# Gate loops of a graph network by units of 1536 columns: one sigmoid per unit into SBUF, products in place on two engines

## The reference, cut to what matters

```
def _gate(h, q, Wg, bg, Wq, bq):        # B=8, N=32 nodes, L=64 queries, F=768
    hg = jnp.einsum('bnf,gf->bng', h3, Wg[:, :F])
    qg = jnp.einsum('blf,gf->blg', q, Wg[:, F:]) + bg
    attn = jax.nn.sigmoid(hg[:, :, None, :] + qg[:, None, :, :])
    qi = jnp.einsum('bnlf,blf->bnf', attn, q)
    alpha = jax.nn.sigmoid(h3 @ Wq[:, :F].T + qi @ Wq[:, F:].T + bq)
    hn = alpha * jnp.tanh(qi) + (1.0 - alpha) * h3
```

## Time and profile before

| what | value |
|---|---|
| time, median of 3 runs (lowest, highest) | 1493.0 us (1488.9, 1496.4) |
| the profiled execution: span from the first to the last instruction | 1493.6 us |
| PE busy, share of the span | 1374.3 us, 92% |
| DVE busy | 992.7 us, 66% |
| ACT busy | 773.0 us, 52% |
| POOL busy | 225.7 us, 15% |
| first gate loop, first selection to the last sums copied | 155.1 to 273.3 us of the span |
| second gate loop | 375.6 to 493.8 us |

### The profile page before, as it was taken

The page is one execution under the profiler, slowest core; times in us unless marked ns, Lnnn a source line. Parts: engine busy times, 40 slices in busy tenths (PEclk is TensorE's granted clock), DMA queues, the critical chain, the costliest instruction groups (busy, mean ns, idle before and its releaser), DMA issues.

```text
span 1493.6 us, 24053 instructions
## 1 busy us (share of the span) xinstructions
PE 1374.3 (92%) x10000; PEld 1165.3 (78%) x10000; DVE 992.7 (66%) x1776; ACT 773.0 (52%) x1245; POOL 225.7 (15%) x115
## 2 busy tenths in 40 slices
PE   6999999999999798798789999888999999987998
PEld 5999633699533696588778899778899999976976
DVE  8655777745777756657667677776577767758355
ACT  2346788535788444344554454634345554436343
POOL 4201587100677100102001000001000000000100
PEclk8999999999999899999999899899899999988899
DMA  8174464135364222035324354063355555142100
GB/s 341 45 231 159 127 190 118 64 127 168 119 190 117 75 78 103 0 128 186 111 81 185 127 191 149 22 234 118 115 184 188 171 191 182 61 170 80 69 0 22
DMA packets 30834, 194.81 MB, mean 130 GB/s; under 512 B 4211, under 2 KB 4339, under 8 KB 14726
## 3 DMA queue, kind: packets, MB, share of 16 engines
q1 hardware_dynamic: 30726, 193.27, 38.1%
HBM read 183.03 MB, written 3.93 MB: 125 GB/s over the span
## 4 chain that ended last, share of the span: by engine, by line
PE 73%; DVE 15%; ACT 6%; POOL 3%; issue 1%; DMA 1%; SPq 0%; DVEq 0%; ACTq 0%; POOLq 0%
PE PS L357 58%; PE PS L956 6%; PE PS L965 5%; PE PS L362 3%; DVE WL L300 2%; POOL WK L1151 2%; PE PS L609 1%; PE PS L459 1%; POOL WL L307 1%; DVE SM L534 1%; ACT WH L293 1%; DVE SM L1323 1%; ACT WK L1708 1%; DVE WK L1733 1%; DVE WK L1738 1%
## 5 line engine op out<-in xcount | busy, mean ns | idle before, releaser
L300 DVE TENSOR_TENSOR WL<-w,WH 128x768 fp32r<-128x768 f32 x367 | 349.5, 963 | 216.1 <-ACT WH L293 213.5
L293 ACT ACTIVATE WH<-w 128x768 fp32r<-128x768 f32 x381 | 315.9, 841 | 272.3 <-PE PS L357 264.2
L357 PE MATMUL PS<-XS,WH 128*128 128x256 f32 x2292 | 418.5, 285 | 11.5 <-DVE XS L484 7.1
L357 PEld LDWEIGHTS PS<-XS,WH 128*128 128x128 f32 x2292 | 356.4, 190 | 15.7 <-issue 12.0
L357 PE MATMUL PS<-XS,WL 128*128 128x256 f32 x1146 | 324.2, 283 | 0.0
L357 PEld LDWEIGHTS PS<-XS,WL 128*128 128x128 f32 x1146 | 217.9, 190 | 0.0
L1089 DVE TENSOR_TENSOR WK<-PS,WK 128x1024 f32<-128x1024 f32 x128 | 156.7, 1224 | 55.6 <-ACT PS L1033 54.5
L1151 POOL TENSOR_TENSOR WK<-WK 128x1024 f32<-128x1024 f32 x64 | 152.8, 2392 | 205.7 <-ACT WK L1030 205.7
L357 PE MATMUL PS<-WH,GS 128*128 128x256 f32 x864 | 162.4, 286 | 6.8 <-DVE GS L484 6.7
L1033 ACT ACTIVATE PS<-PS 128x1024 f32<-128x1024 f32 x128 | 129.4, 1011 | 34.8 <-PE PS L956 34.8
L357 PEld LDWEIGHTS PS<-WH,GS 128*128 128x128 f32 x864 | 137.2, 192 | 9.7 <-DVE GS L484 8.1
(11 more groups left out here) (249 smaller groups left out, 2059.1 us busy)
## 6 DMA issues: line engine op xcount, KB each, us to landing
w<-f2W_in SPq DMA_DIRECT2D x40, 1152.0 KB, 5.5
w<-Wrel_in SPq DMA_DIRECT2D x12, 1152.0 KB, 9.0
WK<-qrep_in SPq DMA_DIRECT2D x16, 768.0 KB, 5.4
w<-f1Wi_in SPq DMA_DIRECT2D x8, 1152.0 KB, 5.9
w<-f1Wo_in SPq DMA_DIRECT2D x8, 1152.0 KB, 5.1
w<-f3Wqkv_in SPq DMA_DIRECT2D x6, 1152.0 KB, 13.8
RT<-qg_rows SPq DMA_DIRECT2D x16, 384.0 KB, 6.3
RT<-AS SPq DMA_DIRECT2D x32, 192.0 KB, 6.6
```

The lines of the kernel that those rows point to most:

```text
L293: A.e.activation(w_hi(i), w_raw(i), ACT.Copy).then_inc(*hi("w", i))
L300: V.e.tensor_tensor(w_lo(i), w_raw(i), w_hi(i), ALU.subtract).then_inc(*lo("w", i))
L357: ins = T.e.matmul(o, l, r, start=i == 0 and first, stop=i == n - 1 and last, skip_group_check=lint)
```

## The change

The loop runs over the 64 units instead of the 32 pairs. A unit takes three banks of PSUM, so two units fit (`SP` has two entries of 1536 columns). ScalarE takes one sigmoid of all 1536 columns of the unit, from PSUM to SBUF (`SG` has six entries). VectorE multiplies columns 0 to 1023 in place in SBUF, GpSimd multiplies columns 1024 to 1535 in place in SBUF. A bank is free for the next selection as soon as ScalarE has read it. The sums of a unit are issued four units later, as before (two pairs). The small tasks of VectorE, ScalarE and GpSimd within the loop are moved to the corresponding units, GpSimd's four weight tiles to units 16, 24, 32 and 40.

```
-        PARTS = [((0, 0), (0, 512)), ((0, 1024), (1, 1024)), ((1, 0), (1, 512))]
-        SP = [PS[:, 1024 * (1 + i):1024 * (2 + i)] for i in range(3)]
+        SG = [wk(at + 1536 * u, n=1536) for at in (0, 3072, 14336) for u in range(2)]
+        SP = [PS[:, 1024 + 1536 * i:2560 + 1536 * i] for i in range(2)]
...
+            def select(u):
+                b = u // 8
+                if u % 8 == 0:
+                    T.wait_ge(gin[b % 2], n, b)
+                for i in range(3):
+                    o = bank_at(2 + 3 * (u % 2) + i, ("sg" + n, u, i), (act, "sig" + n, u))
+                    ins = T.e.matmul(o, PK[:, u % 8 * P:(u % 8 + 1) * P], GR[b % 2][:, 512 * i:512 * (i + 1)],
+                                     start=True, stop=True)
+                ins.then_inc(*pe("sel" + n, u))
...
+            for u in range(4, NU):
+                select(u)
+                sums(u - 4)
+                if u % 8 == 6 and u > 8:
+                    turn_q(u // 8 - 1)
...
+            def attend(u):
+                A.wait_ge(pe, "sel" + n, u)
+                if u >= 6:
+                    A.wait_ge(pe, "sum" + n, u - 6)
+                elif u >= 4:
+                    A.wait_ge(pe, "w", qh_ + 5)
+                A.e.activation(SG[u % 6], SP[u % 2], ACT.Sigmoid).then_inc(*act("sig" + n, u))
...
+            def weigh(u):
+                V.wait_ge(act, "sig" + n, u)
+                V.wait_ge(qin[u // 8 % 2], n, u // 8)
+                g = SG[u % 6][:, 0:1024]
+                V.e.tensor_tensor(g, g, GQ[u // 8 % 2][:, 0:1024], ALU.mult).then_inc(*vec("prod" + n, u))
...
+            for u in range(NU):
+                g = SG[u % 6][:, 1024:1536]
+                G.wait_ge(act, "sig" + n, u)
+                G.wait_ge(qin[u // 8 % 2], n, u // 8)
+                G.e.tensor_tensor(g, g, GQ[u // 8 % 2][:, 1024:1536], ALU.mult).then_inc(*pool("prod" + n, u))
+                if u in (16, 24, 32, 40):
+                    feed_pool(qq_ + (u - 8) // 8)
```

More of the change, by code:

```diff
@@ L731, in build @@
         tq = wk(0, k=6, n=256)
-        NPR = 32
-        NSG = 3
-        SG = [wk(at, u=2, n=1536) for at in (0, 3072, 14336)]
-        PARTS = [((0, 0), (0, 512)), ((0, 1024), (1, 1024)), ((1, 0), (1, 512))]
-        SP = [PS[:, 1024 * (1 + i):1024 * (2 + i)] for i in range(3)]
+        NU = 64
+        SG = [wk(at + 1536 * u, n=1536) for at in (0, 3072, 14336) for u in range(2)]
+        SP = [PS[:, 1024 + 1536 * i:2560 + 1536 * i] for i in range(2)]
         GR = [RT[:, 1536 * i:1536 * (i + 1)] for i in range(2)]
@@ L883, in rgcn_vec @@
             feed_vec(t0 + 28)
-        def prod(n, p, q):
-            return pool if q == 1 else vec, "prod" + n, p, q
         def gate_sync(n):
@@ L896, in queries @@
                     o, d = before(b)
-                    for q in range(3):
-                        L.wait_ge(*prod(o, 4 * d + 3, q))
+                    L.wait_ge(vec, "prod" + o, 8 * d + 7)
+                    L.wait_ge(pool, "prod" + o, 8 * d + 7)
                 L.e.dma_start(GQ[b % 2], dr["qrep"][b]).then_inc(*qin[b % 2](n, b))
@@ L903, in rows_q @@
                     o, d = before(b)
-                    L.wait_ge(pe, "sel" + o, 4 * d + 3, 2)
+                    L.wait_ge(pe, "sel" + o, 8 * d + 7)
                 L.wait_ge(qg_out, "qg")
@@ L946, in gate_q, with sums @@
                 ins.then_inc(*pe("w", qh_ + f))
-            def select(p, q):
-                b = p // 4
-                if p % 4 == 0:
+            def select(u):
+                b = u // 8
+                if u % 8 == 0:
                     T.wait_ge(gin[b % 2], n, b)
[L952 to L960, removed]
+                for i in range(3):
[3 more added lines that the diff above has]
+                ins.then_inc(*pe("sel" + n, u))
+            def sums(u):
+                b, j = u // 8, u % 8
                 o = bank_at(b % 2, ("qs" + n, b), (vec, "qa" + n, b)) if j == 0 else ps("qs" + n, b)
-                T.wait_ge(*prod(n, p, 2 * u))
-                T.wait_ge(*prod(n, p, 1))
+                T.wait_ge(vec, "prod" + n, u)
+                T.wait_ge(pool, "prod" + n, u)
                 for g in range(4):
                     ins = T.e.matmul(o[32 * g:32 * (g + 1), 0:384], zsum[:, 28 - 4 * j:60 - 4 * j],
-                                     SG[p % NSG][:, u, 384 * g:384 * (g + 1)], start=j == 0, stop=j == 7,
+                                     SG[u % 6][:, 384 * g:384 * (g + 1)], start=j == 0, stop=j == 7,
                                      skip_group_check=True)
-                ins.then_inc(*pe("sum" + n, p, u))
+                ins.then_inc(*pe("sum" + n, u))
             def turn_q(b):
@@ L982, in gate_pe @@
             gate_q(1)
-            select(0, 0)
-            select(0, 1)
+            select(0)
             gate_q(2)
-            select(0, 2)
+            select(1)
             gate_q(3)
-            select(1, 0)
-            select(1, 1)
+            select(2)
             gate_q(4)
-            select(1, 2)
+            select(3)
             gate_q(5)
[L993 to L1003, removed]
+            for u in range(4, NU):
[3 more added lines that the diff above has]
+                    turn_q(u // 8 - 1)
+            for u in range(NU - 4, NU):
+                sums(u)
             turn_q(7)
@@ L1041, in gate_act @@
             feed_act(qh_ + 6)
[L1042 to L1046, removed]
+            for u in range(NU):
+                attend(u)
+                if u in (7, 9, 11, 13):
+                    feed_act(qq_ + (u - 5) // 2)
             for i, (n0, n1) in enumerate(QI):
@@ L1073, in sum_out @@
             def sum_out(b):
-                V.wait_ge(pe, "sum" + n, 4 * b + 3, 1)
+                V.wait_ge(pe, "sum" + n, 8 * b + 7)
                 if b:
@@ L1102, in gate_vec @@
             feed_vec(qh_ + 6)
[L1103 to L1113, removed]
+            for u in range(NU):
+                weigh(u)
+                if u < 4:
+                    q_out(u + 2)
+                if u % 8 == 2 and u > 8:
+                    sum_out(u // 8 - 1)
+                if u % 8 == 5 and u > 8:
+                    q_in(u // 8 - 1)
             for i, (n0, n1) in enumerate(QI):
@@ L1373, in l0ffn_sync @@
             load_units(fq + 15)
-            load_row("f0bv", 768, (pe, "sel2", 31, 2))
+            load_row("f0bv", 768, (pe, "sel2", 63))
             load_units(fq + 20)
-            load_row("f0bom", 768, (pe, "sel2", 31, 2), parts=2)
+            load_row("f0bom", 768, (pe, "sel2", 63), parts=2)
             load_units(fq + 36)
-            load_row("f0bf2", 768, (pe, "sel2", 31, 2))
+            load_row("f0bf2", 768, (pe, "sel2", 63))
         def l0ffn_pe():
```

## The result

The changed kernel takes 1574.9 us (median of 4 runs, 1570.3 to 1576.8) against 1491.4 for the kernel before on the same chip (4 runs, 1488.9 to 1496.4): ratio 1.0532, 95% interval 1.0478 to 1.0587, that is 71 to 88 us slower. The profiled execution's span grew from 1493.6 to 1571.2, by 77.6. The forecast was 1568, range 1552 to 1592.

The account below looks back on a forecast made before the run. TensorE bound the loop at 1.68 us per unit; afterwards VectorE and GpSimd taking turns in SBUF would, at 2.22. Two loops at +37.2 us each gave 1493.6 + 74.4 = 1568.0 us, range 1552 to 1592.

Parts of the forecast that it names:

- TensorE bound the loop before: Gate loops: TensorE sets 1.68 us per unit, and the change leaves its selections, sums and turns the same.
- Turns: Loop products: VectorE and GpSimd, both reading SBUF, alternate at 1.07 and 1.15 us, together 2.22 per unit.
- Rival 1: Loop products: no turn-taking for these operands, TensorE stays the bound, not slower, 1493 us; chance 0.10.
- Rival 3: Loop products: turns cost 0.1 to 0.3 us more per unit when both queues press, 1580 to 1603; chance 0.12.
- Rival 2: Loops: TensorE falls to half clock, 138 us more if always; chance 0.03 of a fall costing more than 10 us.
- VectorE's supply: Loop queues: three units of supply, 6.7 us, against 3.1 to make the next one; never the bound, costed at nothing.
- the sum: First loop: unit 4's start, 59 units x 2.22 = 131.0, plus 6.8; GpSimd ends at 309.1, L484 at 310.5.
- The size: Each of the two loops grows by 37.2 us, measured to the copy L476.
- the end: Loop end: L484 follows GpSimd's last product, ending 1.41 us later; the open sums are done before it.
- The weight tiles' 6.8 us a loop: GpSimd's four weight tiles (L307) take turns behind VectorE, no longer hidden: 4 x 1.71 = 6.8 us a loop.
- The rest: Outside the two loops: everything behind them stays the same to 1 us.
- The prediction's base of 1493.6: Starting time of the sum: the profiled execution's span before, taken as 0.6 us above the median of runs.

Follow-up runs that it names:

- experiment 6: Changed kernel with the sigmoid split: columns 0 to 1023 stay in PSUM for VectorE, 1024 to 1535 go to SBUF for GpSimd; 1501.9 us, ratio 1.0036.
- 1: Changed kernel with VectorE's product reading its first input from the selection in PSUM, without the sigmoid; 1518.3 us, ratio 1.0164.
- 2: Changed kernel with VectorE multiplying all 1536 columns in SBUF and GpSimd making no product, only its weight tiles; 1522.4 us, ratio 1.0172.
- 3: Changed kernel with columns split 768 to 768 between VectorE and GpSimd; 1614.7 us, ratio 1.0794.
- 8: Changed kernel with columns split 1280 on VectorE to 256 on GpSimd; 1544.8 us in one run.
- 5: Kernel before, pairs kept, with only the sigmoids of parts 0 and 2 moved to SBUF and VectorE multiplying there in place; 1587.4 us, ratio 1.0607.
- experiment 4: Changed kernel with the third selection of each unit issued three times from unit 4 on; 1584.8 us, ratio 1.0581.
- 9: Changed kernel with small extra matmuls before each of the last four sums groups and behind them; 1574.8 us in one run.

## Why the prediction was right

- *TensorE bound the loop before, at 1.68 a unit, and the change gives it nothing.* Held as far as the runs reach: experiment 6 runs the units at the kernel before's pace but for 4 us a loop, and neither it nor any other run got below the loop of before. No run took work off TensorE alone. That units in two slots cost nothing at all, as experiment 6 expected, was a little too good.
- *Turns.* Held within a hundredth each: 1.08 and 1.14 against 1.07 and 1.15, the sum of 2.22 as forecast. Shown by taking the second SBUF input away (1), the other engine away (2), and by two further sizes (3, 8); and making that edit alone costs as much and more (5).
- *Rival 1, no turn-taking,* is out by the same runs. *Rival 3, dearer turns in a long series,* is out: 43 in a row cost what single meetings cost. The Trainium skill, page "SBUF — State Buffer", section "Who interferes with whom", is right on who excludes whom: two SBUF inputs against GpSimd reading SBUF, not one. Read as adding whole durations, it would give 2.52 a unit; the trace has 2.22, since 0.15 us of each instruction stand outside the exclusive part.
- *Rival 2, half clock.* In the steady turns, with TensorE waiting 0.47 of 2.22 us, the granted clock stayed at full. It fell to half four times in each loop, each time within about 5 us of a wait of TensorE behind a weight tile (in loop 1 waits of 3.2, 3.2, 3.2 and 2.3 us from 201.0, 221.5, 241.0 and 260.5, falls at 205.5, 225.9, 243.0 and 263.5). A wait of that length doesn't always bring a fall: in experiment 4 one of 2.3 at 223.2 did, one of 2.7 at 261.9 didn't. Within the loops the falls cost nothing that the sum shows, as TensorE had time to spare (4). At the loop's end the half clock stretched the last sums by 0.66 us, and behind the first loop it cost 1.2 us (9).
- *VectorE's supply, costed at nothing.* It did run dry, though the price was right: behind the third weight tile TensorE, held for 3.2 us, was late, and VectorE stood idle for 2.25 us from 247.37. GpSimd multiplied on without a pause (241.83 to 255.43), and its last product came within 0.3 us of the sum, as the next point shows.
- *The size.* The loop was to grow by 37.2 and grew by 39.1. The term that was mis-sized is the end. I had GpSimd's last product end, L484's turn behind it, and the last sums hidden under it. In the trace L484 came first:

```profile
308.05 2.61 DVE L484 TENSOR_TENSOR AS<-XN,AS 128x1344 fp32r<-128x1344 f32 x1
...
311.93 1.51 PE L959 MATMUL PS<-WK,cp 128*32 128x384 f32 x8 [1.68 <-POOL WK L1126]
313.50 0.56 DVE L476 COPY WK<-PS 128x384 f32<-128x384 f32 x1 [2.83 <-PE PS L959]
```

  It took its turn of 1.41 ahead of GpSimd's last product, which ended at 311.79. Take that turn off and the product ends 142.9 us after unit 4's selection; the sum had 142.6. Then the sums, at half clock in 1.51 us instead of 0.85, could be hidden under nothing: 1.71 from product to copy, where the sum had 0. Together that is the 1.9 us a loop above the forecast. The weight tiles' 6.8 us a loop are inside that agreement.
- *The rest.* The span grew by 77.6 where the sum had 74.4: 3.8 more at the two ends, 1.8 between the loops and 1.0 ahead of them, 3.3 less behind them, where I had taken all three as unchanged. That the 2.8 and the 3.3 nearly cancel is luck.
- *From span to time.* The medians lie 83.5 apart, 5.9 more than the spans. In every run that has both, the time is 1.8 us above its span. By that the profiled execution of the kernel before took about 1495.4 us (an estimate), 4.0 above the median of its four runs, and not 0.6 as the prediction has it from its span; the one of the changed kernel took 1573.0, 1.9 below its median. The prediction's base of 1493.6 was thus 2.2 us above the 1491.4 that the change is measured against, which brought the forecast that much nearer to 1574.9.

## What to carry to other kernels

Before moving an input of a VectorE instruction from PSUM to SBUF, look at what GpSimd does at that time: if both read SBUF and VectorE reads two inputs there, their times add up, and the sum has to be under the pace of the engine that binds. Then the columns belong to the engine that is cheaper per column, here VectorE, and a helper that is twice as dear can make the loop slower than no helper, as it did here (117 us without GpSimd's products, 146 with them). Read such a case by the ends of the instructions: durations include the wait, and no idle time points to it.

## What the runs showed of the hardware

- With two SBUF inputs on VectorE (fp32 product) and GpSimd on SBUF, the two take turns: 1.08 us for 1024 columns on VectorE, 1.14 for 512 on GpSimd, over up to 43 turns in a row. Over 768 to 1280 columns of VectorE and 256 to 768 of GpSimd a further column costs 1.04 and 2.1 ns. With one input in PSUM, all 128 pairs ran free (experiments 1 and 6).
- The part outside the turn is 0.15 us for VectorE (1.23 alone, 1.08 in turn) and 0.14 for GpSimd (1.28 and 1.14).
- TensorE's granted clock stayed at full (2.4 GHz) through units in which TensorE waited 0.47 of 2.22 us. In the changed kernel it fell to half, for 3.4 to 6.8 us, behind each longer wait (2.0 to 3.2 us), with no effect on the pace, because the bound was elsewhere; in experiment 4 one wait in each loop, of 2.7 and 2.8 us, passed without a fall.
- A sigmoid over 1536 columns, three banks of PSUM, takes 1.453 us, one over 512 columns 0.594 (experiment 6) and one over 1024 1.022: 0.84 ns a column throughout.
- The same code behind the second loop took between 993.5 and 1005.4 us in different executions, a spread larger than several of the effects measured here; the three longest had TensorE at half clock for 134 to 135 us there, the others for 99 to 122.
